# A graph attention and convolution kernel: 202 instead of 154 of its 782 columns of source scores come by gather, 580 instead of 628 by matrix products

## What is computed

```python
el = jnp.einsum('nhf,hf->nh', feat_src, attn_l)     # 6250 x 8
er = jnp.einsum('nhf,hf->nh', feat_dst, attn_r)     # 6250 x 8
e = el[src] + er[dst]                               # 100000 x 8
e = jnp.where(e >= 0, e, NEG_SLOPE * e)
exp_e = jnp.exp(e - segment_max(e, dst)[dst])
a = exp_e / jnp.maximum(segment_sum(exp_e, dst)[dst], 1e-16)
rst = segment_sum(feat_v[src] * a[:, :, None], dst)
```

## Time and profile before

| | |
|---|---|
| Runs of the kernel | 4147.86 us median, 4145.99 to 4148.17 |
| Profiled execution, span | 4150.1 us |
| Stretch of the picks in it | 207.55 to about 573.6 us |
| Busy over the span | TensorE 84%, GpSimd 63%, VectorE 55%, ScalarE 43% |
| Instructions | 55488 |

### The profile page before, as it was taken

How to read it: one execution, slowest core, us unless ns; L and a number is a source line. 1 busy time by engine, 2 the same in 40 slices (tenths; PEclk the granted TensorE clock), 3 DMA queues, 4 the chain that set the end, 5 groups by cost and what they waited for, 6 DMA issues and landing times.

```text
span 4150.1 us, 55488 instructions
## 1 busy us (share of the span) xinstructions
PE 3489.9 (84%) x15160; PEld 1694.2 (41%) x15160; DVE 2288.9 (55%) x3880; ACT 1798.3 (43%) x4172; POOL 2607.4 (63%) x2733
## 2 busy tenths in 40 slices
PE   5899988677888888898788888888997788888887
PEld 4499963222233333343333333333443333333332
DVE  6599887677777888885222333333552222333336
ACT  4356522444545555454333443444343333344442
POOL 3654411677777777654777777777106777777775
PEclk9999999899999999999999999999998999999999
DMA  7822325577777777665777777777216777777779
GB/s 285 244 67 61 90 76 208 172 210 210 210 210 211 210 210 211 190 206 190 210 210 210 210 210 210 211 210 210 79 66 211 211 210 210 210 210 210 210 209 351
DMA packets 318375, 804.24 MB, mean 194 GB/s; under 512 B 72905, under 2 KB 98139, under 8 KB 317129
## 3 DMA queue, kind: packets, MB, share of 16 engines
q0 software_dynamic: 199680, 630.72, 52.6%
q1 hardware_dynamic: 88925, 116.91, 8.5%
q10 hardware_dynamic: 29580, 54.49, 3.8%
HBM read 714.52 MB, written 88.21 MB: 193 GB/s over the span
## 4 chain that ended last, share of the span: by engine, by line
PE 34%; POOL 23%; issue 21%; DMA 12%; DVE 6%; SPq 1%; POOLq 1%; DVEq 1%; ACT 1%; ACTq 0%
POOL edge L1280 17%; PE mm L1529 8%; POOL rows_wmat L1280 5%; DMA edge<-h_tab,src_group 5%; DMA rows_wmat<-v_tab,src_group 4%; PE mm L1621 4%; PE sm L1693 4%; PE tr L1621 4%; PE mm L1693 4%; PE sm L1566 3%; PE tr L1693 2%; DVE edge L866 2%; PE tr L1524 1%; DMA ht_tab<-rows_wmat 1%; PE hist_ps L1693 1%
## 5 line engine op out<-in xcount | busy, mean ns | idle before, releaser
L1280 POOL DMA_INDIRECT edge<-h_tab,src_group x1564 | 1484.2, 949 | 708.5 <-issue 447.5
L1436 ACT ACTIVATE hots<-iota,drel 128x128 f32<-128x128 f32 x1760 | 538.0, 388 | 1174.5 <-PE tr L1693 606.9
L1280 POOL DMA_INDIRECT rows_wmat<-v_tab,src_group x782 | 739.4, 945 | 289.2 <-issue 272.4
L1693 PE MATMUL mm<-edge,hots 128*128 x880 | 465.9, 679 | 195.3 <-SPq L1098 189.7
L1693 PE MATMUL sm<-edge,hots 128*128 x880 | 442.6, 650 | 150.5 <-SPq L1098 148.1
L891 DVE TENSOR_TENSOR big<-big,mm 128x512 f32 x220 | 151.4, 688 | 686.6 <-PE tr L1693 668.8
L891 DVE TENSOR_TENSOR big<-big,sm 128x512 f32 x220 | 151.4, 688 | 602.6 <-PE misc L1693 588.6
L1693 PE MATMUL tr<-edge,hots 128*128 x880 | 395.6, 592 | 0.0
L1693 PEld LDWEIGHTS mm<-edge,hots 128*128 128x128 f32 x880 | 183.6, 217 | 470.1 <-issue 469.9
L1529 PE MATMUL mm<-rows_wmat 128*128 128x512 f32 x784 | 356.0, 598 | 0.0
L1693 PEld LDWEIGHTS sm<-edge,hots 128*128 128x128 f32 x880 | 175.8, 207 | 410.3 <-issue 410.0
(11 more groups left out here) (252 smaller groups left out, 4574.0 us busy)
## 6 DMA issues: line engine op xcount, KB each, us to landing
h_tab<-rows_wmat SPq DMA_DIRECT2D x98, 256.0 KB, 2.0
edge<-h_tab,src_group POOLq DMA_INDIRECT x1564, 3.7
rows_wmat<-low_tab SPq DMA_DIRECT2D x157, 128.0 KB
ht_tab<-rows_wmat SPq DMA_DIRECT2D x49, 256.0 KB
big<-ht_tab ACTq DMA_DIRECT2D x49, 256.0 KB, 2.8
v_tab<-rows_wmat ACTq DMA_DIRECT2D x49, 256.0 KB
x_tab<-big SPq DMA_DIRECT2D x49, 256.0 KB, 2.1
rows_wmat<-v_tab,src_group POOLq DMA_INDIRECT x782, 3.7
```

The costliest lines, as they stand in the source:

```text
L1280: pool.indirect_dma_start(ring[:, 2 * u + c, :], None, tab, bass.IndirectOffsetOnAxis(ap=src_group[:, n:n + 1], axis=0)).then_inc(a["rows_ ...
L1436: act.activation(group_hots[:, q % 2, e, :], iota[:, :], ACT.Abs, bias=drel[:, col:col + 1], scale=-1.0).then_inc(a["dist_set"], 1)
L1693: last = pe.matmul(agg_ps[bank][:, :], group_hots[:, q % 2, w % GROUP * 2 + n, :], edge[:, ds(slot[w % OFFS] + n * D, D)], start=(n == 0), ...
```

## The change

```diff
-GCOLS = 154
+GCOLS = 202
 PCOLS = J - GCOLS
...
             def collect(lo, hi):
                 for n in range(lo, hi):
                     if n >= EARLY:
-                        pool.wait_ge(el_masked, n - EARLY + PACED)
+                        pool.wait_ge(el_masked, (n - EARLY) * 2 // 3 + PACED)
```

## The result

The changed kernel takes 4120.14 us (median of four runs, 4114.85 to 4124.8) against 4148.01 us of the kernel before, run beside it (median of four). One of those four took 17647 us, and one of the runs of the kernel before beside the last three experiments 15315 us; such slow runs are left out of every ratio. The ratio is 0.9936, with a 95% interval of 0.9923 to 0.9949: 26.5 us less, between 21 and 32. The forecast was 4121.6 us, 26.3 less.

A forecast was written before the change was run, and what follows sets the result against it. TensorE was taken to bound the picks at 2.213 us per batch. -26.6 us for batches and +0.3 for VectorE, other terms 0, made -26.3: 4147.9 to 4121.6 us, range 4117 to 4130 us.

The forecast's parts named there:

- 12 batches x 2.213 us = -26.6 us: Picks loop on TensorE: 12 batches fewer at 2.213 us each, all on the path, the main term, -26.6 us.
- The direct sample: Trace from 213.74 to 262.43 us: 1.77 indirect DMAs per batch, TensorE busy throughout, VectorE needing 2.05 to 2.08 us per batch.
- 48 gathers at 0 us: GpSimd during the picks: 60 us more work, covered by its 166.1 us of idle time, so 0 us.
- +0.3 us for VectorE, with a bound of +27: VectorE's one-hot trios in the picks: stretched by 1.5 gathers per batch, +0.3 us taken, bounds 0 to +27 us.
- the first rival: Picks: VectorE becomes the bound by a little, +12 us and 4134 us at the middle, 4148 at the bound; chance 0.09.
- The other signs: Picks: 4.43 us per 96 products, 6960 products, end near 547 us, GpSimd idle put to line 690, later stages 26 us earlier.
- The second rival: Picks: each indirect DMA holds VectorE for its whole length, +63 us, 4211 us; chance 0.03.
- The third: After the picks: something due at a fixed time gives the gain back later, some 4140 to 4148 us; chance 0.03.
- Pipeline around the loops, 0 us within 4: 3.2 MB load and stalls at the end of the picks: cost unchanged, 0 us, some 4 us either side.

The follow-up runs named there:

- the last three experiments: Changed kernel with three small stores issued only after the last pick, with 202, 234 and 250 gathers: 4114.77, 4096.73 and 4099.62 us.
- both halves of the change: Changed kernel with only the 154 gathers of before: 4123.14 us, 0.9932; kernel before with gathers released three per two batches: 4148.65 us, 1.0001.
- The runs with two parts of the table: Kernel before and changed kernel, each with 32 products per batch in place of 48 (third score part left out): 4102.89 and 4082.31 us.
- the pace alone: Kernel before, still 157 batches and 154 gathers, with gathers released three per two batches: 4148.65 us, ratio 1.0001.

## Why the prediction was right

- **12 batches x 2.213 us = -26.6 us.** Shown: the batch stayed at 2.213 us, and both halves of the change, run alone, put the gain with the batches (0.9932) and none with the pace (1.0001), and taking products off TensorE shortens the batch. The direct sample, the scatters and gathers back to back ahead of 262 us, was the right row to rest on. That the sum met the ratio within 0.2 us is luck: the interval is 5 us to either side.
- **48 gathers at 0 us.** Right: covered by GpSimd's idle time, which fell by 74 us, for 174.4 - 128.6 = 46 us more of busy time in a window 31 us shorter.
- **+0.3 us for VectorE, with a bound of +27.** No run can tell this value from 0, and the reason was other than mine. I took VectorE's busy time, 95%, for what it needs and left it 0.1 to 0.2 us per batch. The runs with two parts of the table show a need of 1.90 us with either number of gathers, so the first rival had 0.31 us of room against it and was less likely than the 0.09 I gave. The stretches of the trio that I added per gather do not add: with 1.5 gathers per batch VectorE was busy 94.0% in the picks, below the 95 to 98% that I had named as a sign and no more than with one. The other signs came, but for two sizes: GpSimd's idle time is put down to line 690 for 50.9 of its 92.0 us only, since it issues back to back for longer (40.8 us of issue), and the first scan is at 540.3 us and not near 547, by the 3.8 and 3.1 us of the table above. My reading of GpSimd's slices was a little off as well: 5, 4, 4 and 1 tenths, not 4 to 6 and then 1.
- **The second rival**, that the indirect DMA holds VectorE for its whole length, did not occur in the picks. Beside lines 776 and 777 a gather and VectorE do exclude each other, but there the gather is the one that waits. The third did not occur either: from the scans to the end both traces need the same within 0.5 us. That stretch is not so steady in every trace, though: it takes 3576.8 to 3589.1 us over the eleven kernels with three parts, and for the 12 us more of the pace alone I have no reason.
- **Pipeline around the loops, 0 us within 4.** The sum was right, the sentence "the code there is the same" was no reason for it: the stall at the end comes with three small stores, and varied from 2 to 16 us over the kernels. The 4 us that I allowed were too few for that: among the kernels with 145 batches and the stores in their old place the table has 12.3 to 20.1 us. In the profiled pair it gave 3.1 us of the 32.5; in the medians it is hidden in the interval.

## What to carry to other kernels

Where one engine is busy end to end through a loop and the replacement work lies in another engine's idle time, the gain is the number of trips saved times the trip time in the chain; look for a stretch in the same trace that already runs the replacement at the new density, and believe it over a sum of single stretched instructions. An engine that is 95% busy in a loop bound by another may need less: here VectorE was busy 2.01 to 2.10 us per batch and needed 1.90, which only a run that unloads the bound could show. A store of many single elements deserves a look although it has few bytes: three of 512 elements of 4 bytes took about 15 us here, held up the loads behind them and came with gaps on three engines, and they were best put where no load and no pick stood behind.

## What the runs showed that I had not expected

- Three stores of 512 elements of 4 bytes (6 KB in all) delayed the load behind them by about 15 us, and TensorE, VectorE and ScalarE stood still in pieces that wait for nothing the profile shows, 2 to 16 us in all. What they wait for stays open. Gaps on three engines at a time would fit a wait for code, but the trace does not bear it out: in the changed kernel it has no DMA packet at all from 524 to 535 us, and the first packet of a queue of kind "instruction" at 535.2 us, behind the long gaps; in the kernel before that packet is at 566.6 us, and the last gap was over at 564.3.
- The interference of VectorE and an indirect DMA's issue depends on who is first. A gather that meets an instruction of VectorE already under way can be held: 1.60 us behind the start of a one-hot trio, 1.43 beside the scans of line 767, and 4.3 to 4.9 us beside lines 776 and 777, which read two operands of 4256 elements from SBUF. Each time it was over about 0.8 us after VectorE's work was (331.98 after 331.16 us for the trio, 540.86 after 540.04 for line 776). This is what the Trainium skill, SBUF — State Buffer, section Terms, says of the shared port pair ("the loser fully blocks"), and the trace agrees for lines 776 and 777. It does not where the gather is first: it took 0.94 us and stretched the trio by up to 0.28, and the trio did not wait to its end. Nor does it where a gather began 0.42 us into a trio and took 1.01 us, with the trio at 0.87.
